# Order of VectorE's steps in a software-pipelined cross attention: the maximum ahead of the normalisation, the product and the reciprocal ahead of the next inputs

## The chip, the cores and the metric

The kernel runs on one core of one Trainium2 chip. The metric is the device time of one execution in microseconds. The core's engines are TensorE (PE, matrix products; PEld is its weight load), VectorE (DVE), ScalarE (ACT), GpSimd (POOL) and SyncE (SP, which here only issues DMAs). Each runs its own instructions in program order and waits on semaphores for the others.

## The reference

The kernel computes a decoder of four layers, each with an attention part, a cross attention part and a feed-forward part. The change lies in the cross attention of layer 2. Cut to what matters:

```python
def _div_clamp_fp8(x, scale):
    y = jnp.clip(x.astype(jnp.float32) / scale, -448.0, 448.0)
    return _fp8_roundtrip(y.astype(jnp.bfloat16).astype(jnp.float32))

ln_out = _ln(hidden_states, ln_w, ln_b)
q = _ln(linear(ln_out, wq), qln_w, qln_b)        # 16 heads of 128
k = _ln(linear(ln_out, wk), kln_w, kln_b)        # 8 heads
v = linear(ln_out, wv)
core = _gqa(q, k, v)                             # softmax(q k) v, two query heads per key head
qx = _ln(linear(ln_out, wqx), qxln_w, qxln_b)
kx, vx = split(einsum(cond, w_kv_x)); kx = _ln(kx, kxln_w, kxln_b)
xout = _gqa(qx, kx, vx)
cat = concatenate([core, xout])
catq = _div_clamp_fp8(cat, proj_smooth)
return einsum(catq, wproj) * (proj_in_scale * proj_w_scale)
```

The batch is 8 and there are 128 positions of 256 features each.

## The kernel before, in words

The cross attention of layer 2 is a loop of 64 blocks: 8 batch elements, and for each of them 4 groups of heads of the self part and 4 of the cross part. A block has four query heads and two key heads, of 128 x 128 values each. Nothing is scheduled by a planner: each engine has its own loop `for i in range(67)`, written out by hand, and iteration `i` of each works on blocks `i`, `i-1`, `i-2` and `i-3` at different stages. The steps and their lines (of the kernel before):

- TensorE, iteration `i`, in this order: `L2x_project(i)` (q L4190, or L4185 in six of the first 16 blocks, k L4194 or L4196, v L4202 or L4204), `L2x_pTr(i-2)` (transposes of the probabilities, L4230), `L2x_scores(i-1)` (L4222), `L2x_pv(i-2)` (probabilities by values, L4238), `L2x_proj(i-3)` (output projection, L4253), `L2x_qkTr(i)` (transposes of normalised q and k, L4210 and L4214), and once in eight iterations `L2x_uTr` (L4048). `L2x_project(i)` waits for `L2x_norm(i-1)`, `L2x_proj(i-3)` for `L2x_cat(i-3)`, `L2x_qkTr(i)` for `L2x_norm(i)`, `L2x_pv(i-2)` for `L2x_smooth(i-3)`, whose buffer it overwrites.
- ScalarE, iteration `i`: `L2x_qkT(i-1)` (L1995, L1997), `L2x_squares(i)` (L1963, L1965), `L2x_vc(i)` (L1971), `L2x_pTc(i-2)` (L2011), `L2x_rstd(i)` (L1975, L1979), `L2x_exp(i-1)` (L2004, four exponentials with their sums).
- GpSimd, iteration `i`: `L2x_cat(i-3)` (the second half of the rounding, L1336 and L1338), `L2x_prob(i-1)` (probabilities by the reciprocal of their sum, L1330), in four of eight iterations `L2x_quantise_sum` (L1321, L1324, L1326). In the first 19 iterations it also splits weights into bf16 parts, one instruction on 128x1024 values in each of 16 of them (`L2x_rest`, `L2x_lo`, `L2x_qx_rest`, `L2x_qx_lo`: L1288, L1293, L1342, L1346).
- VectorE, iteration `i`: `L2x_smooth(i-3)`, `L2x_resid` (once in eight), `L2x_ss(i)` (sum of squares, L3089), `L2x_norm(i)` (L3095, L3096), `L2x_max(i-1)` (L3100), then the work for the next batch element: at `i % 8 == 0` `L2x_stats`, at 1 `L2x_u`, at 3, 4, 5 and 6 one `L2x_quantise` (L2975, L2979, L2981, L2983); last `L2x_recip(i-1)` (L3106). I call the iterations with `L2x_quantise` quantising iterations; there are 28.

In the kernel before, `L2x_smooth` is four instructions: the product of the attention's output with the reciprocal of the smoothing scale (L3111, out of PSUM), the clip to bf16 (L3115), the exponent's bits (L3117) and the rounding constant (L3119). `L2x_cat` on GpSimd adds and subtracts that constant. `L2x_ss(i)` waits for `L2x_squares(i)`, `L2x_norm(i)` for `L2x_rstd(i)`, `L2x_max(i-1)` for `L2x_scores(i-1)`, `L2x_recip(i-1)` for `L2x_exp(i-1)`, the product for `L2x_pv` of its block.

Of the kernel before, what the change touches and what calls it, by code (L numbers as in the profile page):

```python
# [108 lines left out]
def build_program(nc, dram, out_d):  # L109
# [89 lines left out]
    with stack:  # L199
# [2174 lines left out]
        def _(dve):  # L2374
# [716 lines left out]
            def L2x_norm(i):  # L3091
                dve.wait_ge(rstd_done, L2x_start['rstd'] + i + 1)
                if i > 0:
                    dve.wait_ge(kT_done, i)
                dve.tensor_tensor(qk[:, 0:4, :], L2x_q[:, :, :], rstd[:, 0:4].unsqueeze(2).to_broadcast([128, 4, 128]), ALU.mult)  # L3095
                dve.tensor_tensor(qk[:, 4:6, :], L2x_k[:, :, :], rstd[:, 4:6].unsqueeze(2).to_broadcast([128, 2, 128]), ALU.mult).then_inc(norm_done, 1)  # L3096

            def L2x_max(i):
                dve.wait_ge(score_done, L2x_start['score'] + i + 1)
                dve.tensor_reduce(smax[:, :], L2x_s[:, :, :], AX.X, ALU.max, negate=True).then_inc(max_done, 1)  # L3100

            def L2x_recip(i):
                dve.wait_ge(exp_done, L2x_start['exp'] + i + 1)
                if i > 0:
                    dve.wait_ge(prob_done, L2x_start['prob'] + i)
                dve.reciprocal(erec[:, :], esum[:, :]).then_inc(recip_done, 1)  # L3106

            def L2x_smooth(i):
                c = 4 * (i % 8)
                dve.wait_ge(o_done, L2x_start['o'] + i + 1)  # L3110
                dve.tensor_tensor(ratio[:, :, :], L2x_o[:, :, :], smr[:, c:c + 4].unsqueeze(2).to_broadcast([128, 4, 128]), ALU.mult).then_inc(smooth_done, 1)  # L3111
                dve.wait_ge(smooth_done, i + 1)
                if i > 0:
                    dve.wait_ge(cat_done, L2x_start['cat'] + i)
                dve.tensor_scalar(o16[:, :, :], ratio[:, :, :], 448.0, -448.0, ALU.min, ALU.max).then_inc(oclip_done, 1)  # L3115
                dve.wait_ge(oclip_done, i + 1)
                dve.tensor_scalar(oe16u[:, :, :], o16u[:, :, :], 0x7F80, None, ALU.bitwise_and).then_inc(oexpo_done, 1)  # L3117
                dve.wait_ge(oexpo_done, i + 1)
                dve.tensor_scalar(omagic[:, :, :], oe16[:, :, :], 2.0 ** -6, 1.5 * 2.0 ** 20, ALU.max, ALU.mult).then_inc(omagic_done, 1)  # L3119
# [8 lines left out]

            for i in range(67):
                if i >= 3:  # L3130
                    L2x_smooth(i - 3)
                if i >= 11 and (i - 3) % 8 == 0:
                    L2x_resid((i - 11) // 8)
                if i < 64:
                    L2x_ss(i)
                    L2x_norm(i)
                if 1 <= i < 65:
                    L2x_max(i - 1)
                if i < 56:
                    n, s = i // 8 + 1, i % 8  # L3140
                    if s == 0:
                        L2x_stats(n)
                    if s == 1:
                        L2x_u(n)
                    if s in (3, 4, 5, 6):
                        L2x_quantise(4 * n + s - 3)
                if i == 56:
                    L2f_stats(0)
                if i == 57:
                    L2f_u(0)  # L3150
                if i == 60:
                    L2f_stats(1)
                if i == 62:
                    L2f_u(1)
                if 1 <= i < 65:
                    L2x_recip(i - 1)
            L2x_resid(7)

            dve.wait_ge(resid_done, L2x_start['resid'] + 8)
# [1702 lines left out]
```

## Time and profile before

| | |
|---|---|
| median of 3 runs | 2069.88 us (2068.64 to 2070.6) |
| the profiled execution: its time, its span | 2064.8 us, 2062.9 us |
| busy in the span: PE, DVE, ACT, POOL | 87%, 70%, 53%, 55% |
| the loop of the change: first and last start of L3095 (one per iteration) | 808.3 us, 1315.0 us |
| granted TensorE clock from 816 to 1336 us | 1.00 |

The span is the time from the first to the last instruction of one profiled execution. Times of rows are microseconds from the span's start. Of the whole kernel only the stretch from about 808 to 1336 us runs the loop that the change touches. An instruction's duration in a timeline is from its start to its end, so what it waits for after it has started is in it; what it waits for on a semaphore before it starts is idle time of its engine, shown in square brackets with who ended it.

### The profile page before, as it was taken

What the parts mean: (1) busy time and instruction counts of PE and PEld (TensorE: products, weight loads), DVE (VectorE), ACT (ScalarE), POOL (GpSimd) and SP (SyncE); (2) the same over time, 40 slices, a digit from 0 to 9 for tenths busy, and PEclk for the clock granted to TensorE, in tenths of its full rate; (3) what the DMA queues carried; (4) which work ended last, traced back from release to release, by engine and by line L of the source; (5) the groups of instructions that cost most, each with busy time, mean ns of one, the idle gap of its engine ahead of it and who ended that gap; (6) DMA issues with size and microseconds to landing.
All of it is one profiled execution on the core that took longest, in us unless ns stands there. A gap on an engine that the chain in (4) does not pass through costs nothing.

```text
span 2062.9 us, 29936 instructions
## 1 busy us (share of the span) xinstructions
PE 1795.1 (87%) x10766; PEld 1290.9 (63%) x10810; DVE 1451.8 (70%) x2366; ACT 1092.4 (53%) x2325; POOL 1142.0 (55%) x837
## 2 busy tenths in 40 slices
PE   6777789799999896888999999968888888898999
PEld 4111148555565574666777777767777665677887
DVE  5788853456554584777777777589999887867563
ACT  4444431245323264666666666567767656755443
POOL 3799940112595174766555555499999952123221
PEclk9788899689999998999999999989999989999999
DMA  4211001040200010000000000200000002000000
GB/s 157 58 36 36 0 1 54 26 184 21 109 15 21 0 33 18 14 1 1 1 1 1 1 1 31 93 4 1 1 1 1 26 1 84 1 1 1 6 9 9
DMA packets 20395, 54.79 MB, mean 27 GB/s; under 512 B 8095, under 2 KB 11848, under 8 KB 17944
## 3 DMA queue, kind: packets, MB, share of 16 engines
q1 hardware_dynamic: 20248, 52.88, 7.7%
q8 instruction: 87, 1.43, 0.3%
q14 instruction: 60, 0.49, 0.1%
HBM read 44.48 MB, written 1.05 MB: 22 GB/s over the span
## 4 chain that ended last, share of the span: by engine, by line
PE 51%; DVE 21%; ACT 12%; POOL 7%; issue 7%; DMA 0%; DVEq 0%; POOLq 0%; ACTq 0%
DVE sbuf L2446 4%; PE psum L4355 3%; PE psum L4013 3%; ACT sbuf L2004 2%; PE psum L3996 2%; PE psum L3988 2%; PE psum L3641 2%; PE psum L4253 2%; PE psum L4190 2%; ACT sbuf L2100 2%; POOL sbuf L1152 1%; DVE sbuf L3117 1%; PE psum L4663 1%; PE psum L4345 1%; POOL sbuf L1338 1%
## 5 line engine op out<-in xcount | busy, mean ns | idle before, releaser
L1388 POOL TENSOR_TENSOR sbuf<-sbuf 128x1035 f32<-128x1035 f32 x128 | 245.1, 1945 | 0.9 <-ACT sbuf L2068 0.9
L4355 PE MATMUL psum<-sbuf 128*128 128x128 f32 (+1 forms) x1024 | 144.2, 291 | 56.2 <-ACT sbuf L2100 41.4
L2100 ACT ACTIVATE sbuf<-sbuf 128x1001 f32<-128x1001 f32 (+1 forms) x128 | 142.0, 1142 | 84.9 <-DVE sbuf L3241 60.9
L4355 PEld LDWEIGHTS psum<-sbuf 128*128 128x128 f32 (+1 forms) x1024 | 125.9, 152 | 77.5 <-ACT sbuf L2100 55.5
L1330 POOL TENSOR_TENSOR sbuf<-sbuf 128x512 f32<-128x512 f32 x64 | 66.7, 1042 | 172.8 <-DVE sbuf L3106 172.8
L1152 POOL TENSOR_TENSOR sbuf<-sbuf 128x1024 f32<-128x1024 f32 x64 | 149.8, 2353 | 17.0 <-DVE sbuf L2446 17.0
L2446 DVE TENSOR_TENSOR_SCAN sbuf<-psum,sbuf 128x1024 f32<-128x1024 f32 x64 | 144.8, 2278 | 12.6 <-ACT psum L1534 7.4
L2004 ACT ACTIVATE sbuf<-psum,sbuf 128x128 f32<-128x128 f32 x256 | 90.4, 365 | 107.2 <-DVE sbuf L3100 107.2
L3233 DVE SCALAR_TENSOR_TENSOR psum<-sbuf,psum 128x1024 f32<-128x1024 f32 (+1 forms) x96 | 122.3, 1274 | 23.0 <-PE psum L4345 16.5
L3587 PE MATMUL psum<-sbuf 96*128 96x512 bf16 x256 | 82.1, 432 | 60.5 <-DVE sbuf L2446 32.4
L1534 ACT ACTIVATE psum<-psum,sbuf 128x1016 f32<-128x1016 f32 x64 | 69.0, 1082 | 119.7 <-PE psum L3587 119.7
L4253 PE MATMUL psum<-sbuf 128*128 128x256 bf16 x768 | 94.9, 273 | 30.9 <-POOL sbuf L1338 30.5
L3241 DVE TENSOR_TENSOR sbuf<-psum,sbuf 128x1024 f32<-128x1024 f32 (+1 forms) x96 | 116.4, 1212 | 3.3
L4253 PEld LDWEIGHTS psum<-sbuf 128*128 128x128 bf16 x768 | 70.8, 98 | 60.2 <-POOL sbuf L1338 51.4
L3587 PEld LDWEIGHTS psum<-sbuf 96*128 96x128 bf16 x256 | 18.8, 102 | 137.1 <-DVE sbuf L2446 62.4
L1336 POOL TENSOR_TENSOR sbuf<-sbuf 128x512 f32<-128x512 bf16 x64 | 74.5, 1164 | 46.2 <-DVE sbuf L3119 44.5
L1462 POOL TENSOR_TENSOR sbuf<-sbuf 128x1024 f32<-128x1024 f32 x16 | 30.8, 1944 | 120.1 <-DVE sbuf L3437 120.1
L4190 PE MATMUL psum<-sbuf 128*128 128x512 bf16 x304 | 81.7, 387 | 6.1 <-issue 3.9
L1338 POOL TENSOR_TENSOR sbuf<-sbuf 128x512 bf16<-128x512 f32 x64 | 81.3, 1270 | 5.0
L3620 PE MATMUL psum<-sbuf 128*32 128x512 f32 x256 | 78.5, 746 | 3.9 <-POOL sbuf L1152 3.9
L1396 POOL TENSOR_TENSOR sbuf<-sbuf 128x1024 f32<-128x1024 f32 (+1 forms) x32 | 68.7, 2148 | 21.0 <-DVE sbuf L3233 21.0
L3095 DVE TENSOR_TENSOR sbuf<-psum,sbuf 128x512 f32<-128x512 f32 x64 | 44.2, 691 | 50.6 <-ACT sbuf L1979 50.6
(696 smaller groups left out, 5023.0 us busy)
## 6 DMA issues: line engine op xcount, KB each, us to landing
sbuf<-sbuf SPq DMA_DIRECT2D x50, 128.0 KB, 2.4
sbuf<-w_gu_d SPq DMA_DIRECT2D x2, 2048.0 KB, 11.4
sbuf<-w_p_d SPq DMA_DIRECT2D x8, 512.0 KB, 3.6
sbuf<-w_qkv_d SPq DMA_DIRECT2D x3, 768.0 KB, 4.3
sbuf<-w_e_d SPq DMA_DIRECT2D x1, 2048.0 KB, 9.2
sbuf<-w_dn_d SPq DMA_DIRECT2D x1, 2048.0 KB, 18.7
sbuf<-w_q_d SPq DMA_DIRECT2D x1, 2048.0 KB, 7.9
sbuf<-w_qx_d SPq DMA_DIRECT2D x1, 2048.0 KB, 12.4
```

Of the source, the lines that this page charges most:

```text
L1152: pool.tensor_tensor(L0a_hc[i % 4][:, :], L0a_hs[i % 2][:, :], L0a_Cr[g % 4][:, :], ALU.mult).then_inc(hc_done, 1)
L1338: pool.tensor_tensor(cat16[:, :, :], cat[:, :, :], omagic[:, :, :], ALU.subtract).then_inc(cat_done, 1)
L1388: pool.tensor_tensor(P_r[g % 7][:, :, :], rows.unsqueeze(2).to_broadcast([128, 23, 45]), cols.unsqueeze(1).to_broadcast([128, 23, 45]), AL ...
L2004: last = act.activation(prob[:, h, :], L2x_s[:, h, :], ACT.Exp, bias=smax[:, h:h + 1], accum_out=esum[:, h:h + 1])
L2100: act.activation(Q_r[g % 6][:, 0:w], Q_r[g % 6][:, 0:w], ACT.Silu, scale=q8_p[n % 2][:, h:h + 1]).then_inc(silu_done, 1)
L2446: dve.tensor_tensor_scan(L0a_hs[i % 2][:, :], L0a_dAf[i % 2][:, :], L0a_us[i % 3][:, :], 0.0, ALU.mult, ALU.add).then_inc(scan_done, 1)
L3233: dve.scalar_tensor_tensor(M[:, 0:w], Pf_r[g % 7][:, o:o + w], t8_p[n % 2][:, h, 7:8], zps[:, 0:w], ALU.is_ge, ALU.mult).then_inc(mask_don ...
L3241: dve.tensor_tensor(Q_r[g % 6][:, 0:w], Mps[:, 0:w], Pf_r[g % 7][:, o:o + w], ALU.mult).then_inc(prod_done, 1)
L3587: last = pe.matmul(out[:, 512 * h:512 * h + 512], rows, L0a_stack[g % 4][0:96, a, 512 * h:512 * h + 512], start=True, stop=True)
L4190: last = pe.matmul(L2x_q[:, :, :], xs16[n % 2][:, part, c, :], (L2x_q_part, L2x_qx_part)[part](p, g)[:, c, :], start=c == 0 and p == 0, st ...
L4253: last = pe.matmul(L2x_out[:, :], cat16[:, h, :], w_p3[p][:, 4 * (i % 8) + h, :], start=i % 8 == 0 and h == 0 and p == 0, stop=i % 8 == 7 ...
L4355: last = pe.matmul(Gps[0:m, c, :], Q_r[g % 6][:, 128 * c:128 * c + m], ident[:, :], start=h == 0 and c % 4 == 0, stop=h == 7, skip_group_c ...
```

## The change

On VectorE alone, two things are done. `L2x_smooth` is cut in two: the product stays in `L2x_smooth`, and the clip, the exponent's bits and the constant become `L2x_magic`. And the order within an iteration is new. No instruction is added or removed, no wait is added or removed, and no other engine's program is touched; no DMA is issued in the moved steps.

```diff
@@ L2x_smooth(i) @@
                 dve.wait_ge(o_done, L2x_start['o'] + i + 1)
                 dve.tensor_tensor(ratio[:, :, :], L2x_o[:, :, :], smr[:, c:c + 4].unsqueeze(2).to_broadcast([128, 4, 128]), ALU.mult).then_inc(smooth_done, 1)
+
+            def L2x_magic(i):
                 dve.wait_ge(smooth_done, i + 1)
                 if i > 0:
                     dve.wait_ge(cat_done, L2x_start['cat'] + i)
@@ the loop @@
             for i in range(67):
                 if i >= 3:
-                    L2x_smooth(i - 3)
+                    L2x_magic(i - 3)
                 if i >= 11 and (i - 3) % 8 == 0:
                     L2x_resid((i - 11) // 8)
                 if i < 64:
                     L2x_ss(i)
-                    L2x_norm(i)
                 if 1 <= i < 65:
                     L2x_max(i - 1)
+                if i < 64:
+                    L2x_norm(i)
+                if 2 <= i < 66:
+                    L2x_smooth(i - 2)
+                if 1 <= i < 65:
+                    L2x_recip(i - 1)
                 if i < 56:
                     n, s = i // 8 + 1, i % 8
                     ...
                 if i == 62:
                     L2f_u(1)
-                if 1 <= i < 65:
-                    L2x_recip(i - 1)
```

The `...` stands for the work for the next batch element, which is unchanged. In the changed kernel the clip, the exponent's bits and the constant stand two lines further down: L3117, L3119 and L3121.

VectorE in iteration 2, which has no quantisation, from the normalisation up to the constant; before:

```order
L3095 TENSOR_TENSOR sbuf<-psum,sbuf 128x512
L3096 TENSOR_TENSOR sbuf<-psum,sbuf 128x256
L3100 TENSOR_REDUCE sbuf<-psum 128x4
L3106 RECIPROCAL sbuf<-sbuf 128x4
L3111 TENSOR_TENSOR sbuf<-psum,sbuf 128x512
L3115 TENSOR_SCALAR sbuf<-sbuf 128x512
L3117 TENSOR_SCALAR sbuf<-sbuf 128x512
L3119 TENSOR_SCALAR sbuf<-sbuf 128x512
```

The same iteration in the changed kernel:

```order
L3100 TENSOR_REDUCE sbuf<-psum 128x4
L3095 TENSOR_TENSOR sbuf<-psum,sbuf 128x512
L3096 TENSOR_TENSOR sbuf<-psum,sbuf 128x256
L3111 TENSOR_TENSOR sbuf<-psum,sbuf 128x512
L3106 RECIPROCAL sbuf<-sbuf 128x4
L3117 TENSOR_SCALAR sbuf<-sbuf 128x512
L3119 TENSOR_SCALAR sbuf<-sbuf 128x512
L3121 TENSOR_SCALAR sbuf<-sbuf 128x512
```

The maximum (L3100) now stands before the normalisation, and the product (L3111) before the reciprocal (L3106), so that the clip follows the reciprocal directly.

VectorE in a quantising iteration; before:

```order
L3095 TENSOR_TENSOR sbuf<-psum,sbuf 128x512
L3096 TENSOR_TENSOR sbuf<-psum,sbuf 128x256
L3100 TENSOR_REDUCE sbuf<-psum 128x4
L2975 TENSOR_TENSOR sbuf<-sbuf 128x256
L2979 TENSOR_SCALAR sbuf<-sbuf 128x256
L2981 TENSOR_SCALAR sbuf<-sbuf 128x256
L2983 TENSOR_SCALAR sbuf<-sbuf 128x256
L3106 RECIPROCAL sbuf<-sbuf 128x4
L3111 TENSOR_TENSOR sbuf<-psum,sbuf 128x512
L3115 TENSOR_SCALAR sbuf<-sbuf 128x512
L3117 TENSOR_SCALAR sbuf<-sbuf 128x512
L3119 TENSOR_SCALAR sbuf<-sbuf 128x512
```

The same in the changed kernel:

```order
L3100 TENSOR_REDUCE sbuf<-psum 128x4
L3095 TENSOR_TENSOR sbuf<-psum,sbuf 128x512
L3096 TENSOR_TENSOR sbuf<-psum,sbuf 128x256
L3111 TENSOR_TENSOR sbuf<-psum,sbuf 128x512
L3106 RECIPROCAL sbuf<-sbuf 128x4
L2975 TENSOR_TENSOR sbuf<-sbuf 128x256
L2979 TENSOR_SCALAR sbuf<-sbuf 128x256
L2981 TENSOR_SCALAR sbuf<-sbuf 128x256
L2983 TENSOR_SCALAR sbuf<-sbuf 128x256
L3117 TENSOR_SCALAR sbuf<-sbuf 128x512
L3119 TENSOR_SCALAR sbuf<-sbuf 128x512
L3121 TENSOR_SCALAR sbuf<-sbuf 128x512
```

The four quantising instructions (L2975 to L2983) stood between the maximum and the reciprocal; now they stand between the reciprocal and the clip.

## Rows read from the trace of the kernel before

**Rows 1.** Busy time in 64 us of the loop's later part (view of windows).
```profile
core 0: us, PE busy (x) PEld busy (x) DVE busy (x) ACT busy (x) POOL busy (x), PEclk, DMA share, GB/s
1016.00:1080.00 64.00, 61.16 (x397) 49.44 (x403) 48.28 (x96) 42.45 (x141) 33.94 (x32) 1.00 0.00 1
```

**Rows 2.** Waits, 888 to 1330 us: total, times, longest.
```profile
DVE sbuf L3106 <- ACT sbuf L2004: 51.2, 55, 1.6
DVE sbuf L3095 <- ACT sbuf L1979: 42.8, 55, 1.0
PE psum L4253 <- POOL sbuf L1338: 23.4, 32, 2.4
```

**Rows 3.** Timeline of VectorE: the normalisation in iterations 1, 17, 18, 20, 32, 40.
```profile
816.06 0.69 DVE L3095 TENSOR_TENSOR sbuf<-psum,sbuf 128x512 f32<-128x512 f32 x1 [0.61 <-ACT sbuf L1979]
...
957.43 0.69 DVE L3095 TENSOR_TENSOR sbuf<-psum,sbuf 128x512 f32<-128x512 f32 x1 [0.61 <-ACT sbuf L1979]
...
966.27 0.69 DVE L3095 TENSOR_TENSOR sbuf<-psum,sbuf 128x512 f32<-128x512 f32 x1 [0.61 <-ACT sbuf L1979]
...
983.37 0.69 DVE L3095 TENSOR_TENSOR sbuf<-psum,sbuf 128x512 f32<-128x512 f32 x1 [0.61 <-ACT sbuf L1979]
...
1076.79 0.69 DVE L3095 TENSOR_TENSOR sbuf<-psum,sbuf 128x512 f32<-128x512 f32 x1 [0.99 <-ACT sbuf L1979]
...
1138.76 0.69 DVE L3095 TENSOR_TENSOR sbuf<-psum,sbuf 128x512 f32<-128x512 f32 x1 [0.99 <-ACT sbuf L1979]
```

**Rows 4.** Chain that ended last: TensorE through iteration 34, without a wait.
```profile
1087.19 1.24 PE psum L4190 x5
...
1090.59 0.89 PE psum L4222 x8
...
1092.41 1.48 PE psum L4253 x12
1093.89 0.44 PE psum L4210 x4
1094.32 0.22 PE psum L4214 x2
```

**Rows 5.** Timeline, reciprocal of iteration 34, then quantising iteration 35.
```profile
1094.88 0.18 DVE L3106 RECIPROCAL sbuf<-sbuf 128x4 f32<-128x4 f32 x1 [1.57 <-ACT sbuf L2004]
...
1099.44 0.69 DVE L3095 TENSOR_TENSOR sbuf<-psum,sbuf 128x512 f32<-128x512 f32 x1 [0.94 <-ACT sbuf L1979]
...
1100.38 0.68 DVE L3100 TENSOR_REDUCE sbuf<-psum 128x4 f32<-128x512 f32 x1
...
1102.63 0.18 DVE L3106 RECIPROCAL sbuf<-sbuf 128x4 f32<-128x4 f32 x1 [0.32 <-ACT sbuf L2004]
...
1102.89 1.04 POOL L1330 TENSOR_TENSOR sbuf<-sbuf 128x512 f32<-128x512 f32 x1 [3.05 <-DVE sbuf L3106]
...
1103.42 0.79 DVE L3115 TENSOR_SCALAR sbuf<-sbuf 128x512 bf16<-128x512 f32 x1
...
1103.89 0.85 POOL L1321 TENSOR_TENSOR sbuf<-sbuf 128x256 f32<-128x256 bf16 x1
...
1104.25 0.65 DVE L3117 TENSOR_SCALAR sbuf<-sbuf 128x512 uint16<-128x512 uint16 x1
...
1104.82 0.73 POOL L1326 TENSOR_TENSOR sbuf<-sbuf 128x256 bf16<-128x256 f32 x1
...
1104.93 0.90 DVE L3119 TENSOR_SCALAR sbuf<-sbuf 128x512 f32<-128x512 bf16 x1
...
1108.48 1.48 PE L4253 MATMUL psum<-sbuf 128*128 128x256 bf16 x12 [1.07 <-POOL sbuf L1338]
```

**Rows 6.** Timeline, VectorE's iteration 16: GpSimd's 128x1024 split.
```profile
953.19 2.16 POOL L1346 TENSOR_TENSOR sbuf<-sbuf 128x1024 bf16<-128x1024 f32 x1
```

**Rows 7.** Single lines over the loop: durations in ns, min/median/max.
```profile
L3115 DVE TENSOR_SCALAR sbuf<-sbuf x64: 426/793/1429, 828.9 to 1328.6; 128x512 bf16<-128x512 f32 x64
...
L3117 DVE TENSOR_SCALAR sbuf<-sbuf x64: 293/646/2108, 829.7 to 1329.0; 128x512 uint16<-128x512 uint16 x64
...
L2975 DVE TENSOR_TENSOR sbuf<-sbuf x32: 411/415/707, 790.1 to 1248.5; 128x256 f32<-128x256 f32 x32
...
L4185 PE MATMUL psum<-sbuf x24: 592/592/596, 836.9 to 935.9; 128*128 128x512 f32 x24
```

## The prediction, made before the changed kernel ran

> **What bounds the loop now.** I read the windows first. In the later part of the loop TensorE is busy 61.16 of 64 us and VectorE 48.28 [rows 1]: TensorE is nearly full, but not quite. The chain that ended last shows what a full TensorE means: iteration 34 runs from 1087.19 to the end of its last transposes at 1094.54 without a wait, so 7.35 us, about 7.40 with the step to the next [rows 4]. Against this stand the measured periods. From iteration 32 to 40 the normalisation moves from 1076.79 to 1138.76, 61.97 us or 7.75 an iteration; from 1 to 20 it takes 983.37 - 816.06 = 167.3 us, 8.81 an iteration; from 17 to 18 it is 8.84 [rows 3]. So the floor is some 59.3 us for eight iterations, and the loop pays 2.6 us over it later on and far more in the first 20.
>
> The waits say who holds TensorE up: the output projection waits for GpSimd's second half of the rounding (23.4 us in all), and GpSimd is late because VectorE is. VectorE in turn stands still twice in an iteration with nothing else to do: 42.8 us in 55 iterations for the inverse deviation ahead of the normalisation, 51.2 us for the exponentials ahead of the reciprocal [rows 2]. VectorE's own circle (squares, wait, normalisation, maximum, exponentials, reciprocal, rounding, next squares) thus sets the period, not its busy time. In quantising iteration 35 the constant ends at 1104.93 + 0.90 = 1105.83, 6.39 us after the normalisation began, and the projection starts 2.65 us after that, having waited 1.07 [rows 5].
>
> One more thing is in the rows. The clip, the exponent's bits and the constant don't have one duration. The bits take 0.29 us at best, 0.65 in the median, 2.11 at most; the clip 0.43, 0.79 and 1.43 [rows 7]. They are long when GpSimd works: in iteration 35 the clip ends 0.28 us after GpSimd's L1330 (1103.93), the bits 0.16 after L1321 (1104.74), the constant 0.28 after L1326 (1105.55) [rows 5]; in iteration 16 GpSimd's 128x1024 split takes 2.16 us [rows 6], about the longest time of the bits. I read it as one excluding the other. The product L2975 (two SBUF inputs) does it too, 0.41 against 0.71 [rows 7]. The Trainium skill, "SBUF — State Buffer", section "SBUF: two separate sides", says that a VectorE instruction that uses both ports, or has two SBUF inputs, and a GpSimd instruction take a shared pair of ports in turn, whoever starts first for its whole length; the trace agrees.
>
> **The change, step by step.** No work is added, so all depends on the circles. Times below count from R, the end of the reciprocal.
>
> *Maximum first.* It needs the scores, not the deviation, and takes 0.68 us of the 0.94 us in which VectorE waited [rows 5]. *Product before the reciprocal.* The normalisation occupies 0.94 us up to the next instruction, the product some 0.61 (reciprocal and product together are 0.79, 1102.63 to 1103.42 [rows 5]); together 1.55, and the exponentials keep the reciprocal waiting 1.57 after the maximum in an iteration with no filler [rows 5]. Both are hidden. The risk is that the product waits for `L2x_pv(i-2)`, with the reciprocal queued behind it. TensorE ends that 0.93 us after the scores (1091.48 to 1092.41 [rows 4]), and the product starts 1.6 us after them: free, with 0.7 us to spare. The normalisation starts later, but ends some 1.7 us after the scores, while TensorE still has 0.93 + 1.48 us to go before it needs it.
>
> With this VectorE's own circle no longer holds both idle times. The circle that counts now goes over GpSimd and TensorE and takes two iterations: scores(i-1), maximum, exponentials, reciprocal, rounding(i-2), `cat`, projection, transposes, project(i+2), scores(i+1). Its pieces: scores to R 0.05 + 0.68 + 1.57 + 0.18 = 2.48; R to the end of the constant m; from there to the projection 2.65; projection and transposes 1.48 + 0.44 + 0.22 + 0.04 = 2.18; project to the end of the scores 1091.48 - 1087.19 = 4.29 [rows 4, 5]. Period = (11.60 + m) / 2.
>
> - *No quantisation, no split.* The clip follows the reciprocal at once, before GpSimd's L1330 can begin, and runs in 0.43; L1330 then ends at 1.35, the bits at 1.54, the constant at m = 2.0. Period 6.8, under TensorE's 7.40: TensorE sets it.
> - *Quantisation.* Product L2975 to 0.33, L1330 to 1.3, L2979, L2981, L2983 to 2.0, clip to 2.4, then in turns L1321 to 3.0, bits to 3.15, L1326 to 3.8, constant to 4.1. So m = 4.1, where before it was 1105.83 - 1102.81 = 3.02: the four moved instructions no longer lie in the wait for the exponentials. Period 7.85. If L1330 wins the first turn m is 3.8 and the period 7.70.
> - *128x1024 split, no quantisation* (10 iterations): the split begins at 1.54, ends at 3.5, the constant at 3.8. Period 7.7 to 7.85, in place of 8.84 to 9.2.
> - *Split and quantisation* (3 to 6, and 11): `cat` starts only behind both, near 6.0, and the projection at 8.55. Period (2.48 + 8.55 + 2.18 + 4.29)/2 = 8.75, and with q by L4185 (4 x 0.59 in place of 1.24 [rows 4, 7], half of the 1.1 counting) 9.3.
>
> The sum over iterations 1 to 20: ten periods at 7.85 (78.5), four at 9.3 (37.2), two at 8.4 for L4185 (16.8), two for iteration 11 and its follower (17.5), one more at 7.85: 157.9 against 167.3, so -9.4 us. Each later group of eight: four at 7.85 and four at 7.40 and 0.2 for L4048, 61.2 against 61.97, -0.8; with four and a half groups -3.6. The last, unquantised iterations are at TensorE's pace already: -0.4. Together -13.4 us. Profiled execution 2064.8 -> 2051.4 (span 2062.9 -> 2049.5); the median of the runs lies 5.1 above the profiled time, so 2069.9 - 13.4 = 2056.5.
>
> By the nearest rows without the taking of turns (every instruction at its shortest) m would be 2.3 with a quantisation, and the period 6.95, under 7.40. The page's rule, in which GpSimd and VectorE exclude each other, speaks against this change in its quantising iterations, where it puts more of VectorE's instructions against L1330.
>
> **The rivals.**
> 1. *TensorE sets every period.* For it: the shortest durations [rows 7]. Against: turns seen in iteration 35. 62 iterations at 7.40, 6.6 for L4185 and 1.5 for L4048 make 467, the loop now takes 499: -32, giving 2038. Chance 0.08.
> 2. *Later quantising iterations gain nothing and the first 20 only half*, because GpSimd's split takes its turn ahead of the bits and the constant both: -4 to -6, 2064 to 2066. 0.15.
> 3. *The change doesn't reach the end:* VectorE's waits move and the projection waits as before, 2070 ± 4. For it: with quantisation the new period 7.85 is close to the present ones. 0.10.
> 4. *Slower, by the moved quantisation.* m is the place. Each us more in m costs 0.5 us in 28 iterations, 14 us. The gain of 13.4 is gone when m passes 5.05, which needs one more full GpSimd instruction (1.04 us) between the reciprocal and the constant. At m = 5.4 the time is 2075. Against: GpSimd has only L1330, L1321 and L1326 there. 0.09.
>
> **How the numbers follow.** The forecast circle has 0.58, its own range 2049 (m 3.8, splits cheaper) to 2062. A difference of 0.2% is 4.1 us, about what this measurement can tell. Faster: 0.58 + 0.08 + 0.13 of rival 2 and a little of 3 = 0.80; within 0.2%: 0.11; slower 0.09. The range leaves out most of rival 1 and of rival 4: 2044 to 2069.
>
> **What would show it.** Right: from the normalisation of iteration 1 to that of 20 some 158 us, 20 to 56 in steps of 7.4 and 7.85; the wait before L3095 near nothing, the maximum right after the squares; the clip 0.43 us in iterations without quantisation; in quantising ones the constant ending 4.1 us after the reciprocal, with projections that still wait a few tenths. Wrong: the product waiting for L4238, the reciprocal pushed off by it, the constant more than 5 us behind the reciprocal, or an unchanged wait before L4253.

## The result, and the profile after

| | before | after |
|---|---|---|
| median, with lowest and highest | 2068.82 us, 8 runs (2059.31 to 2070.6) | 2056.23 us, 8 runs (2045.5 to 2058.16) |
| profiled execution: time, span | 2064.8 us, 2062.9 us | 2055.56 us, 2053.8 us |
| from the span's start to the normalisation of iteration 1 | 816.1 us | 820.2 us |
| the loop, normalisation of iteration 1 to that of 63 | 499.0 us | 480.6 us |
| from there (iteration 63) to the end of the span | 747.9 us | 753.0 us |

The changed kernel is faster by 0.58%: the ratio of the times is 0.9942, with a 95% interval of 0.9922 to 0.9963. The loop alone gained 18.4 us, and 5.1 us of them were lost again behind it. The two profiled spans differ by only 9.1 us, because the stretch ahead of the loop, which the change does not touch, took 4.1 us more in the changed kernel's. That stretch varies from execution to execution of one kernel: 811.3 us at a mean granted clock of 0.92 in the trace of max_first below, 822.2 us at 0.90 in that of max_first_again, the same program. Where an iteration stands is read, as in [rows 3], from the start of the normalisation in VectorE's timeline; in the changed kernel these are iterations 1, 20, 32, 40 and 63.

```profile
820.15 0.68 DVE L3095 TENSOR_TENSOR sbuf<-psum,sbuf 128x512 f32<-128x512 f32 x1
...
977.07 0.68 DVE L3095 TENSOR_TENSOR sbuf<-psum,sbuf 128x512 f32<-128x512 f32 x1
...
1068.48 0.68 DVE L3095 TENSOR_TENSOR sbuf<-psum,sbuf 128x512 f32<-128x512 f32 x1
1129.11 0.68 DVE L3095 TENSOR_TENSOR sbuf<-psum,sbuf 128x512 f32<-128x512 f32 x1
...
1300.76 0.68 DVE L3095 TENSOR_TENSOR sbuf<-psum,sbuf 128x512 f32<-128x512 f32 x1
```

Iterations 1 to 20 take 156.9 us (before 167.3, [rows 3]), 32 to 40 take 60.63 (before 61.97). The square bracket of [rows 3], the wait of the normalisation for the inverse deviation, is gone from the rows: the maximum now fills that time. VectorE's wait in an iteration has moved to the maximum itself, which waits for the scores. In the view of waits, 880 to 1316 us (total, times, longest), this reads so:

```profile
DVE sbuf L3100 <- PE psum L4227: 35.3, 46, 1.1
...
PE psum L4258 <- POOL sbuf L1338: 14.5, 18, 2.7
```

The projection's wait for GpSimd (L4258, in the kernel before L4253, 23.4 us in 32 cases [rows 2]) is down to 14.5 us in 18. The chain that ended last shows both kinds of iteration. First, from 1078.02, an iteration that TensorE sets, without a wait; then the quantising iteration 35, where the chain leaves TensorE for VectorE's maximum when the scores are there (1089.95), and comes back to TensorE only with a later projection:

```profile
1078.02 1.24 PE psum L4195 x5
...
1083.25 1.31 PE psum L4258 x12
...
1084.99 0.22 PE psum L4219 x2
...
1089.95 0.70 DVE sbuf L3100
```

The TensorE iteration takes 1085.21 - 1078.02 + 0.05 = 7.24 us. I had taken 7.40: the projection was 1.48 us in [rows 4] and is 1.31 here, where `cat` is ready before TensorE comes to it. The iteration of [rows 4] was not quite free of waits: the timeline of the weight loads has the projection's first one begin only with its matmuls, at 1092.40, after 0.39 us of waiting for L1338. The rounding of iteration 35 in the timeline of VectorE and GpSimd is the forecast sequence:

```profile
1092.21 0.18 DVE L3106 RECIPROCAL sbuf<-sbuf 128x4 f32<-128x4 f32 x1
1092.31 0.41 DVE L2975 TENSOR_TENSOR sbuf<-sbuf 128x256 f32<-128x256 f32 x1
...
1092.47 1.15 POOL L1330 TENSOR_TENSOR sbuf<-sbuf 128x512 f32<-128x512 f32 x1 [3.23 <-DVE sbuf L3106]
...
1092.75 1.02 DVE L2979 TENSOR_SCALAR sbuf<-sbuf 128x256 bf16<-128x256 f32 x1
...
1094.28 0.42 DVE L3117 TENSOR_SCALAR sbuf<-sbuf 128x512 bf16<-128x512 f32 x1
1094.44 0.78 POOL L1321 TENSOR_TENSOR sbuf<-sbuf 128x256 f32<-128x256 bf16 x1 [0.82 <-DVE sbuf L2983]
1094.73 0.65 DVE L3119 TENSOR_SCALAR sbuf<-sbuf 128x512 uint16<-128x512 uint16 x1
...
1095.30 0.73 POOL L1326 TENSOR_TENSOR sbuf<-sbuf 128x256 bf16<-128x256 f32 x1
1095.41 0.90 DVE L3121 TENSOR_SCALAR sbuf<-sbuf 128x512 f32<-128x512 bf16 x1
```

The constant (L3121) ends at 1096.31, 3.92 us after the reciprocal (1092.39); L2979, whose shortest duration in this trace is 0.29 us, takes 1.02 because it started behind L1330.

### The profile page after: what moved, and what is told of

The parts are those of the page before. It is cut to its first block, busy times and chain, and to the rows that moved or that the text cites. A ratio compares the mean times of both kernels' runs of the same rounds, so it can differ in the third digit from the quotient of the medians.

```text
span 2053.8 us, 29936 instructions
## 1 busy us (share of the span) xinstructions
PE 1803.1 (88%) x10766; PEld 1306.0 (64%) x10810; DVE 1465.0 (71%) x2366; ACT 1098.5 (53%) x2325; POOL 1145.8 (56%) x837
## 4 chain that ended last, share of the span: by engine, by line
PE 60%; DVE 17%; ACT 9%; POOL 7%; issue 6%; DMA 0%; DVEq 0%; POOLq 0%; ACTq 0%
DVE sbuf L2446 4%; PE psum L4360 4%; PE psum L4258 3%; PE psum L3993 3%; PE psum L4001 3%; PE psum L4018 3%; PE psum L4195 2%; PE psum L3646 2%; PE psum L4227 2%; PE psum L4668 1%; ACT sbuf L2004 1%; ACT sbuf L2100 1%; POOL sbuf L1388 1%; PE psum L4369 1%; PE psum L4350 1%
## 5 line engine op out<-in xcount | busy, mean ns | idle before, releaser
L4360 PE MATMUL psum<-sbuf 128*128 128x128 f32 (+1 forms) x1024 | 150.5, 300 | 54.4 <-ACT sbuf L2100 39.6
L4360 PEld LDWEIGHTS psum<-sbuf 128*128 128x128 f32 (+1 forms) x1024 | 132.8, 158 | 74.0 <-ACT sbuf L2100 52.8
L1330 POOL TENSOR_TENSOR sbuf<-sbuf 128x512 f32<-128x512 f32 x64 | 72.2, 1128 | 131.7 <-DVE sbuf L3106 129.8
L4258 PE MATMUL psum<-sbuf 128*128 128x256 bf16 x768 | 95.8, 275 | 20.2 <-POOL sbuf L1338 20.0
L4258 PEld LDWEIGHTS psum<-sbuf 128*128 128x128 bf16 x768 | 72.9, 98 | 44.0 <-POOL sbuf L1338 32.1
L1336 POOL TENSOR_TENSOR sbuf<-sbuf 128x512 f32<-128x512 bf16 x64 | 74.4, 1162 | 37.2 <-DVE sbuf L3121 35.5
L3089 DVE TENSOR_REDUCE sbuf<-sbuf 128x6 f32<-128x768 f32 x64 | 60.8, 950 | 44.8 <-ACT sbuf L1965 44.7
L1338 POOL TENSOR_TENSOR sbuf<-sbuf 128x512 bf16<-128x512 f32 x64 | 81.2, 1269 | 5.0
```

Of the source, the lines that this page charges most:

```text
L1338: pool.tensor_tensor(cat16[:, :, :], cat[:, :, :], omagic[:, :, :], ALU.subtract).then_inc(cat_done, 1)
L4258: last = pe.matmul(L2x_out[:, :], cat16[:, h, :], w_p3[p][:, 4 * (i % 8) + h, :], start=i % 8 == 0 and h == 0 and p == 0, stop=i % 8 == 7 ...
L4360: last = pe.matmul(Gps[0:m, c, :], Q_r[g % 6][:, 128 * c:128 * c + m], ident[:, :], start=h == 0 and c % 4 == 0, stop=h == 7, skip_group_c ...
```

## The experiments

I call the parts A (the maximum ahead of the normalisation), B (`L2x_smooth` cut in two, with the product ahead of the clip by one iteration) and C (the reciprocal ahead of the next inputs' work). The changed kernel is A + B + C. All lengths in this table are read as above, each from one profiled execution; times in us. m is, as in the prediction, the time from the end of the reciprocal to the end of the constant, and a circle is a closed chain of waits through the engines that fixes the loop's period. The ratio is to the kernel before, run on the same chip.

| kernel | parts | median | ratio, 95% interval | 1 to 20 | 20 to 56 | 56 to 63 | loop | loop to end |
|---|---|---|---|---|---|---|---|---|
| before | none | 2068.82 | | 167.3 | 279.3 | 52.3 | 499.0 | 747.9 |
| changed | A B C | 2056.23 | 0.9942 [0.9922, 0.9963] | 156.9 | 272.8 | 50.9 | 480.6 | 753.0 |
| after_again | A B C | 2057.06 | 0.9942 [0.9926, 0.9959] | 157.0 | 272.8 | 50.9 | 480.7 | 753.0 |
| max_first | A | 2045.79 | 0.9874 [0.9848, 0.9899] | 154.2 | 268.8 | 50.9 | 473.9 | 749.0 |
| max_first_again | A | 2045.16 | 0.9872 [0.9850, 0.9895] | 154.2 | 268.8 | 50.9 | 473.9 | 749.1 |
| recip_last | A B | 2048.26 | 0.9893 [0.9871, 0.9915] | 156.4 | 271.3 | 50.9 | 478.6 | 747.7 |
| no_max_first | B C | 2100.98 | 1.0145 [1.0122, 1.0168] | 174.1 | 301.8 | 53.6 | 529.6 | 748.3 |
| product_early | B | 2063.06 | 0.9966 [0.9954, 0.9978] | 165.5 | 274.2 | 51.4 | 491.1 | 749.4 |
| quantise_early | A B C, quantisation moved | 2084.68 | 1.0065 [1.0044, 1.0085] | 172.5 | 290.0 | 50.9 | 513.4 | 746.8 |
| bits_twice | A B C, one instruction more | 2059.66 | 0.9951 [0.9934, 0.9967] | 160.7 | 276.6 | 50.9 | 488.2 | 747.9 |
| mixed | A, and B where nothing is quantised | 2044.26 | 0.9870 [0.9849, 0.9891] | 155.6 | 268.8 | 50.9 | 475.4 | 747.5 |
| leave_later | A B C, 24 instructions behind the loop | 2052.76 | 0.9912 [0.9896, 0.9929] | 156.9 | 272.8 | 50.9 | 480.6 | 748.7 |

### One part at a time: max_first, recip_last, no_max_first

max_first is the kernel before with A alone:

```diff
                 if i < 64:
                     L2x_ss(i)
-                    L2x_norm(i)
                 if 1 <= i < 65:
                     L2x_max(i - 1)
+                if i < 64:
+                    L2x_norm(i)
```

> The kernel before with one part of the change: the maximum ahead of the normalisation; product, clip, bits and constant stay together, the reciprocal stays last. Theory (the circle scores, maximum, reciprocal, cat, projection over two iterations): VectorE's own circle loses its wait before the normalisation; in quantising iterations the reciprocal ends about 3.2 us after the scores and the constant 3.0 after it, period 7.7; without quantisation TensorE's pace. From the normalisation of iteration 1 to that of 63 some 481 us against 499 before, so nearly the whole gain of the change, -15 to -19 us. Rival (each moved step brings its own share): about half, some -6 to -10 us.

recip_last is the changed kernel without C:

```diff
                 if 2 <= i < 66:
                     L2x_smooth(i - 2)
-                if 1 <= i < 65:
-                    L2x_recip(i - 1)
                 if i < 56:
                     ...
+                if 1 <= i < 65:
+                    L2x_recip(i - 1)
```

> The changed kernel with the reciprocal again behind the quantisation (maximum first and early product stay). Theory: reciprocal 3.6 us after the scores in quantising iterations, constant 2.4 after it, but cat has to wait for GpSimd's two quantising additions, projection 5.6 after the reciprocal: period 7.8, against 7.76 in the changed kernel. So no difference of over 2 us from the changed kernel, 1 to 63 some 482 us. Rival (the reciprocal's place matters, since it starts GpSimd): 8 us or more worse than the changed kernel.

no_max_first is the changed kernel without A:

```diff
                 if i < 64:
                     L2x_ss(i)
+                    L2x_norm(i)
                 if 1 <= i < 65:
                     L2x_max(i - 1)
-                if i < 64:
-                    L2x_norm(i)
```

> The changed kernel with the normalisation again ahead of the maximum; product early, reciprocal ahead of the quantisation. Theory: VectorE's own circle is whole again (squares, wait, normalisation, maximum, exponentials, reciprocal 3.37 us after the normalisation's start, then 3.9 to the constant in quantising iterations, then 1.47 to the next normalisation): 8.7 us in each quantising iteration, 7.3 in the others. 1 to 63 some 509 us, 10 us more than before: about +0.5%. Rival (the other moves help by themselves): -3 to -8 us against before.

A alone takes 25.1 us from the loop, more than the whole change does and 6 us more than the most I expected of it: its four quantising iterations from 27 to 31 take 30.31 us, 7.58 each in place of the expected 7.7, and the others go at 7.24. B on top of it costs 4.7 us and C 2.0 more (473.9, 478.6, 480.6). In the medians A alone is ahead of the changed kernel by 10 to 12 us, and recip_last by 8 to 9, more than the loop gives, because the stretch behind the loop is shorter than in the changed kernel as well (749.0 and 747.7 us against 753.0; see below). Its quantising iteration 35 in the timeline of VectorE and GpSimd shows why:

```profile
1076.86 0.69 DVE L3100 TENSOR_REDUCE sbuf<-psum 128x4 f32<-128x512 f32 x1 [0.80 <-PE psum L4223]
1077.46 0.68 DVE L3095 TENSOR_TENSOR sbuf<-psum,sbuf 128x512 f32<-128x512 f32 x1
...
1078.84 0.29 DVE L2979 TENSOR_SCALAR sbuf<-sbuf 128x256 bf16<-128x256 f32 x1
...
1079.64 0.17 DVE L3106 RECIPROCAL sbuf<-sbuf 128x4 f32<-128x4 f32 x1
...
1079.89 1.04 POOL L1330 TENSOR_TENSOR sbuf<-sbuf 128x512 f32<-128x512 f32 x1 [3.38 <-DVE sbuf L3106]
1080.42 0.80 DVE L3115 TENSOR_SCALAR sbuf<-sbuf 128x512 bf16<-128x512 f32 x1
...
1081.93 0.90 DVE L3119 TENSOR_SCALAR sbuf<-sbuf 128x512 f32<-128x512 bf16 x1
```

The quantisation lies in the time of the exponentials, GpSimd stands still, and L2979 takes 0.29 us in place of 1.02. The reciprocal is later for it, 1079.81 - 1076.82 = 2.99 us after the scores in place of 2.48, but the constant follows it by 3.02 in place of 3.9. The circle of the prediction with these two in it is 2.99 + 3.02 + 2.65 + 2.18 + 4.29 = 15.13 us for two iterations; the normalisations of iterations 35 and 37 (1077.46 and 1092.62) start 15.16 apart.

In recip_last the same circle reads so in the chain (from the scores of a quantising iteration to its projection):

```profile
1101.91 0.03 DVE sbuf L3100
...
1105.29 0.18 DVE sbuf L3106
...
1105.54 1.13 POOL sbuf L1330
1106.67 0.68 POOL sbuf L1321
...
1107.43 0.79 POOL sbuf L1326
1108.22 1.13 POOL sbuf L1336
...
1110.74 1.48 PE psum L4258 x12
```

With the product and the quantisation both ahead of it, the reciprocal ends 3.59 us after the scores (1105.46 - 1101.87). The clip runs early and the constant is ready 2.18 us behind the reciprocal, but that is of no use: `cat` (L1336) begins only when GpSimd has done L1330, L1321 and L1326, after some 2.7 us. From the scores to `cat` it is 2.99 + 3.10 = 6.09 us with A, 3.59 + 2.72 = 6.31 with A and B, and 2.48 + 4.00 = 6.48 with all three (1092.39 to 1096.39). With the 2.56 + 2.18 + 4.29 us of the rest, two iterations should take 15.12, 15.34 and 15.51 us; measured are 15.16, 15.38 and 15.53. From iteration 20 to 56 there are ten such circles of two iterations, so these differences make 2.2 us for B and 1.7 for C, where 2.5 and 1.5 are measured.

Without A, the order B + C is 30.6 us slower in the loop than the kernel before, where I had expected 10: the product stands between the maximum and the reciprocal, and the reciprocal ahead of the quantisation, so that a quantising iteration has both of VectorE's waits and the whole quantisation one behind the other. Most quantising iterations take 8.74 us, as expected (8.7); what I had too low are others: of those expected at 7.3, 24 to 25 takes 8.30 and 26 to 27 takes 8.10. Its timeline has the wait in front of the normalisation in full again, here in iterations 32 and 40, 67.29 us apart:

```profile
1096.32 0.69 DVE L3095 TENSOR_TENSOR sbuf<-psum,sbuf 128x512 f32<-128x512 f32 x1 [0.98 <-ACT sbuf L1979]
...
1163.61 0.69 DVE L3095 TENSOR_TENSOR sbuf<-psum,sbuf 128x512 f32<-128x512 f32 x1 [0.99 <-ACT sbuf L1979]
```

### The product alone: product_early

The kernel before with `L2x_smooth` cut in two, `L2x_magic(i-3)` first and `L2x_smooth(i-2)` behind the maximum; the reciprocal stays last, the normalisation first.

```diff
                 if i >= 3:
-                    L2x_smooth(i - 3)
+                    L2x_magic(i - 3)
                 ...
                 if 1 <= i < 65:
                     L2x_max(i - 1)
+                if 2 <= i < 66:
+                    L2x_smooth(i - 2)
```

> The kernel before with the product alone moved: behind the maximum, ahead of quantisation and reciprocal; normalisation still ahead of the maximum. Theory: VectorE's own circle is 3.37 to the reciprocal's end, 1.84 (2.2 with quantisation) to the constant and 1.47 to the next normalisation, 6.7 to 7.0, below TensorE's pace, so this alone also frees it; but with quantisation cat comes behind GpSimd's two additions, 5.5 after the reciprocal, and the circle through the projection is (3.45 + 5.5 + 2.18 + 4.55)/2 = 7.85. 1 to 63 some 483 us, -14 to -16 us. Rival (only the maximum's place matters): within 3 us of the kernel before.

B without A gains 7.9 us in the loop, half of what I expected of it. In unquantised iterations the constant ends 1.84 us after the reciprocal in place of 2.19. In quantising ones the reciprocal comes 0.2 us later, and the constant 2.17 us after it in place of 3.02 (of the 20 from iteration 19 on, one still has 3.02). So B gains while VectorE still waits for the deviation, and loses 4.7 us with A in place, where, as above, the late reciprocal costs more than B gives.

### Where the quantisation should lie: quantise_early

The changed kernel with the quantisation moved from behind the reciprocal to behind the constant, ahead of the squares, so that m has no quantisation in it:

```diff
                 if i >= 11 and (i - 3) % 8 == 0:
                     L2x_resid((i - 11) // 8)
+                if i < 56 and i % 8 in (3, 4, 5, 6):
+                    L2x_quantise(4 * (i // 8 + 1) + i % 8 - 3)
                 if i < 64:
                     L2x_ss(i)
                 ...
-                    if s in (3, 4, 5, 6):
-                        L2x_quantise(4 * n + s - 3)
```

> The changed kernel with the four quantising instructions moved from behind the reciprocal to behind the constant, ahead of the sum of squares, where VectorE stands idle 0.7 to 1.2 us for the squares and 0.8 for the scores. Theory: the constant then ends some 2.5 us after the reciprocal instead of 3.9, cat is held by GpSimd's own additions to a projection 5.6 us after the reciprocal, period of quantising iterations about 7.3 instead of 7.76. 1 to 63 some 471 us against 480.6: 9 us better than the changed kernel. Rival (the sum of squares becomes late, and with it the inverse deviation and the normalisation): no gain or a loss of some us.

I expected 471 us for the loop; it takes 513.4, 32.8 us more than in the changed kernel. m is 2.20 us in quantising iterations, no longer than expected; the loss is at the new place. The timeline of both engines at the new place:

```profile
1063.38 0.94 DVE L2975 TENSOR_TENSOR sbuf<-sbuf 128x256 f32<-128x256 f32 x1
1064.00 1.35 POOL L1336 TENSOR_TENSOR sbuf<-sbuf 128x512 f32<-128x512 bf16 x1
...
1064.36 1.14 DVE L2979 TENSOR_SCALAR sbuf<-sbuf 128x256 bf16<-128x256 f32 x1
...
1065.43 1.26 POOL L1338 TENSOR_TENSOR sbuf<-sbuf 128x512 bf16<-128x512 f32 x1
1065.54 1.24 DVE L2981 TENSOR_SCALAR sbuf<-sbuf 128x256 uint16<-128x256 uint16 x1
...
1066.81 0.29 DVE L2983 TENSOR_SCALAR sbuf<-sbuf 128x256 f32<-128x256 bf16 x1
1067.02 0.95 DVE L3089 TENSOR_REDUCE sbuf<-sbuf 128x6 f32<-128x768 f32 x1
```

Three instructions of 0.41, 0.29 and 0.23 us at their shortest take 0.94, 1.14 and 1.24, as each has one of GpSimd's in front of it, and the squares come 1067.02 - 1063.38 = 3.64 us after the quantisation began. The period there is 9.05 us (the maximum starts at 1058.83 and at 1067.88 in this trace). This is the statement of the Trainium skill, "SBUF — State Buffer", section "SBUF: two separate sides", that GpSimd's instructions and those of VectorE that use both ports or have two SBUF inputs take a shared pair of ports in turn; the trace agrees, with 1.24 against 0.23 us for L2981. I had used it for the moved rounding and not for this place.

### The size of m: bits_twice

The changed kernel with the exponent's bits taken twice, one behind the other (not shown: one wait behind the loop counts the 64 more):

```diff
                 dve.tensor_scalar(oe16u[:, :, :], o16u[:, :, :], 0x7F80, None, ALU.bitwise_and).then_inc(oexpo_done, 1)
-                dve.wait_ge(oexpo_done, i + 1)
+                dve.wait_ge(oexpo_done, 2 * i + 1)
+                dve.tensor_scalar(oe16u[:, :, :], o16u[:, :, :], 0x7F80, None, ALU.bitwise_and).then_inc(oexpo_done, 1)
+                dve.wait_ge(oexpo_done, 2 * i + 2)
```

> The changed kernel with the exponent's bits taken twice in each iteration (the same result), which adds some 0.3 us to VectorE between the reciprocal and the constant, everywhere. Theory (the circle over two iterations, and only where its sum exceeds TensorE's pace): 0 in iterations without quantisation after number 20 (there is 0.8 us of slack), about 0.15 in quantising ones, so eight iterations 61.2 instead of 60.6 and 1 to 63 some 5 us more, 485 us. Rival (VectorE's busy time counts in each iteration): 0.3 in each of 62, 19 us more.

From iteration 13 on m grows by 0.33 us (3.90 to 4.24 with a quantisation, 1.84 to 2.17 without). A usual group of eight, 24 to 32, grows from 60.36 to 61.24 us. These 0.88 us are about five times half of 0.34: the four quantising iterations and the one right behind them (31 to 32, 7.24 to 7.46), which closes the last circle of two. The other unquantised iterations keep their length (24 to 26 at 7.24 each), so TensorE sets them, and the last seven take 50.9 as before. This is the prediction's rule that a microsecond in m costs half of one in quantising iterations and nothing in the others, but for the one iteration behind each group. The stretch from 32 to 40 grows by 0.61 only, because in the changed kernel it is longer than its neighbours (60.63): m is 4.19 there in iteration 36 by itself. From 20 to 56 all this makes the measured 3.8 us. In iterations 3, 4, 5 and 11, where GpSimd splits weights too, m is 6.04 us in place of 3.9, and 12 to 13 is shorter (9.97 in place of 11.49, see the last section); the net of 1 to 20 is another 3.8. The loop so costs 7.6 us more where I expected 5, and not the rival's 19.

### The better order in each iteration: mixed

recip_last, but with the product behind the reciprocal, as in the kernel before, in the quantising iterations:

```diff
+                late = i < 56 and i % 8 in (3, 4, 5, 6)
-                if 2 <= i < 66:
+                if 2 <= i < 66 and not late:
                     L2x_smooth(i - 2)
                 ...
                 if 1 <= i < 65:
                     L2x_recip(i - 1)
+                if late:
+                    L2x_smooth(i - 2)
```

> A version meant to be best: maximum first, reciprocal last (behind the quantisation, which so stays in the wait for the exponentials), the product ahead of the reciprocal only in iterations without quantisation. Theory (circle over two iterations): with a 128x1024 split and no quantisation the constant comes 3.64 after the reciprocal, as in the changed kernel, instead of 4.01 in the kernel with the maximum first alone; with quantisation 3.0, as there. So iteration 1 to 20 some 152 us against 154.2, the rest alike (268.8 and 50.9), 1 to 63 some 472 us against 473.9 and 480.6; median 2044 us. Rival (mixing costs the product's slot once at each change of order): 474 to 476 us.

The loop takes 475.4 us, 1.5 more than with A alone; from 20 to 56 the two are equal (268.8). I expected 472, with 2 us saved by B while GpSimd splits weights. It saves only 0.3 there, and 1.7 are lost in one place: iterations 11 to 13 take 18.75 us against 17.02 in max_first, with 11.48 against 9.09 from 12 to 13. By its median mixed is not to be told from max_first. No version beat A alone by more than the measurement can tell.

### Why the end came later: after_again, max_first_again, leave_later

after_again and max_first_again are the same programs again, to see whether the loop and the stretch behind it repeat.

> The changed kernel once more, beside the others on one chip. In the first comparison 7 of 8 of its runs had a granted clock of 0.939 or 0.940 over the whole kernel (2055 to 2058 us), one had 0.947 (2045.5 us). Theory (the clock of the stretches outside the loop varies from run to run and is no work of the change): here the clock spreads as with the kernel before, 0.944 to 0.950, and the time is 2050 us. Rival (the change lowers the clock outside the loop): 0.940 and 2056 us again. The loop takes 480.6 us from the normalisation of iteration 1 to that of 63 in either case.

> The kernel before with the maximum first alone, once more. In the loop it is 6.7 us shorter than the changed kernel (473.9 against 480.6). If the clock outside the loop is the same for both, the difference of the medians is 7 us; if the changed kernel's clock is lower by itself, 10 to 12 us as in the first comparisons.

They do: 480.7 and 473.9 us in the loop, 753.0 and 749.1 behind it. My theory for after_again, 2050 us with a clock that spreads as before, fell: all its six runs stand at 0.938 to 0.940 and 2056 to 2057 us, as the rival said, and its median is 11.9 us above max_first_again's. So the 5.1 us that the changed kernel loses behind the loop are no accident of one execution. No instruction there is different. The windows of the changed kernel behind the loop (columns as in [rows 1]):

```profile
1300.00:1700.00 400.00, 329.57 (x2159) 285.13 (x2158) 338.51 (x513) 254.31 (x383) 337.42 (x182) 0.91 0.05 16
1700.00:2053.00 353.00, 324.90 (x2554) 257.42 (x2554) 221.75 (x354) 193.23 (x351) 88.42 (x72) 0.98 0.03 10
```

The same two stretches behind the loop of the kernel before:

```profile
1315.00:1715.00 400.00, 324.41 (x2166) 277.39 (x2164) 340.66 (x517) 257.31 (x386) 337.39 (x182) 0.93 0.06 20
1715.00:2062.00 347.00, 321.94 (x2550) 255.31 (x2546) 218.77 (x349) 189.60 (x346) 88.41 (x72) 0.99 0.02 5
```

The granted clock (third number from the end) is 0.91 and 0.98 where it was 0.93 and 0.99, and TensorE is busy longer with about as many matmuls. leave_later tests whether the work or the moment matters: it is the changed kernel with 24 more instructions of VectorE between the loop and its last addition (not shown: one later wait counts them).

```diff
+            dve.wait_ge(omagic_done, 64)
+            for r in range(24):
+                dve.wait_ge(oexpo_done, 64 + r)
+                dve.tensor_scalar(oe16u[:, :, :], o16u[:, :, :], 0x7F80, None, ALU.bitwise_and).then_inc(oexpo_done, 1)
+            dve.wait_ge(oexpo_done, 88)
             L2x_resid(7)
```

> The changed kernel with 24 repeats of the last block's exponent bits before the last residual addition, so that the loop's end comes some 4 us later and all behind it moves by that; the loop itself stays at 480.6 us. In the changed kernel's two profiles the stretch from the normalisation of iteration 63 to the end takes 753.0 us, in all others 747 to 749, at a higher clock. Theory (the clock behind the loop depends on when the loop is left): the stretch takes 749 + 4 = 753 us or less, mean clock 0.944 or more, median within 2 us of the changed kernel's 2057 although 4 us of work were added. Rival (the changed kernel's loop, with its power, lowers the clock behind it, whenever it is left): 753 + 4 = 757 us, clock 0.939, median 2061.

The first instruction of the next stage on GpSimd, in the timelines of the changed kernel and of leave_later:

```profile
1327.31 5.75 POOL L1388 TENSOR_TENSOR sbuf<-sbuf 128x1035 f32<-128x1035 f32 x3 [0.92 <-ACT sbuf L2068]
```

```profile
1330.95 1.93 POOL L1388 TENSOR_TENSOR sbuf<-sbuf 128x1035 f32<-128x1035 f32 x1 [0.91 <-ACT sbuf L2068]
```

It comes 26.55 us after the last normalisation in the one (1300.76) and 28.36 in the other (1302.59). The work was added and the stage does start 1.8 us later, not the 4 that I had expected. Yet from there to the end the changed kernel takes 2053.8 - 1327.31 = 726.5 us and leave_later 2051.3 - 1330.95 = 720.4, on the same instructions, with this clock:

```profile
1302.00:1702.00 400.00, 323.15 (x2158) 276.70 (x2157) 349.56 (x539) 255.92 (x384) 337.29 (x182) 0.93 0.06 18
1702.00:2051.00 349.00, 322.71 (x2554) 255.79 (x2554) 219.62 (x352) 191.01 (x349) 88.41 (x72) 0.98 0.02 7
```

A kernel with more to do is 3.5 to 4.3 us faster in the median, where I expected it within 2 us of the changed one; the intervals of the ratios just overlap. The rival, that the changed loop lowers the clock behind it whenever it is left, gave 757 us from the last normalisation to the end; it is 748.7. bits_twice, which also does more, has 747.9. So the 5 us are not what the change does to the later stages, which run the same instructions: they go with the clock granted there.

What brings that clock about these runs don't show. It is not the delay of the next stage alone: in mixed the same instruction of GpSimd also comes 26.55 us after the last normalisation (1322.07), and from there to the end it takes 720.9 us. It is not the time since the span's start alone either: max_first and max_first_again leave the loop at 1285.2 and 1296.1 us and both take 749 us from there.

## Why the prediction was right, and where only its numbers met

The time, 2056.23 us, is the forecast 2056.5, inside the range, with the forecast sign. The terms behind it were further off, and that the total met is luck: the loop gained 5.0 us more than forecast, and 5.1 us were lost behind it, where the forecast had nothing.

- **What bounds the loop:** right. The two waits of VectorE set the period, and A, which fills one of them, is worth 25.1 us alone; without it the rest makes the kernel slower.
- **"Maximum first", "product before the reciprocal", both hidden:** the first is right. Of the second I asked only whether the product waits or delays the reciprocal, and it does neither (R is 2.48 us after the scores, as worked out). What I didn't weigh is what the whole change would be without it. The parts B and C are a loss of 6.7 us in the loop beside A: B delays the reciprocal where something is quantised, and C puts the quantisation's 2 us behind it, where L1330 lengthens L2979 to 1.02. The term m = 4.1 had this in it, so the forecast didn't suffer; I never asked whether one part spoke against another.
- **The two-iteration circle:** right. m was forecast at 4.1 or 3.8 and is 3.9 in quantising iterations (but 5.0 in iteration 12 and 4.19 in 36); it was forecast at 2.0 and is 1.84 to 2.3 in the others of the later part. Two quantising iterations take (2.48 + 3.90 + 2.65 + 2.18 + 4.29) = 15.50 us by the formula and 7.24 + 8.29 = 15.53 in the trace. max_first, and bits_twice behind iteration 20, moved as the formula says.
- **TensorE's pace of 7.40:** mis-sized; it is 7.24. The projection's 1.48 us of [rows 4] is what it takes when its weight load has waited for `cat`; with `cat` there in time it is 1.31.
- **The sum:** the terms were -9.4, -3.6 and -0.4 us; measured are -10.4, -6.5 and -1.4. Of the 5.0 us that the forecast gave too little, 3.9 lie behind iteration 20. Some 2.9 of them are TensorE's pace in the 24 unquantised iterations there, and 1.1 the 19 quantising ones at 7.79 in place of 7.85. The other 1.0, in the first 20, is a net: iterations 3 to 6 take 35.6 us in place of 37.2, iteration 11 and its follower 18.7 in place of 17.5, where the granted clock fell once (last section), and the rest 0.5 less.
- **What lies behind the loop:** taken as unchanged, and 5.1 us longer at a lower granted clock. This undid the surplus almost exactly. Without the loss behind the loop the prediction would have stood some 5 us too high, still inside its range.
- **The profiled execution and the median:** the forecast put the profiled time at 2051.4 us and it is 2055.56; the median is 0.7 us above it and not 5.1. The 4.1 us that the stretch ahead of the loop took more make most of that difference: the 5.1 belonged to one execution of the kernel before, so that the profiled time's miss is not one of the circle. One of the eight runs of the changed kernel took 2045.5 us at a granted clock of 0.947, the seven others 2055 to 2058 at 0.939 or 0.940. There is no trace of it. The two profiled executions of max_first and max_first_again lie as far apart, 2035.91 us at 0.951 and 2046.97 at 0.944, and theirs is ahead of the loop (811.3 and 822.2 us); so that run is no evidence on the loss behind the loop.
- **The rivals:** 1 (TensorE sets every period, 2038) fell on the 8.29 us of every second quantising iteration. 2 fell: iterations 20 to 56 gained 6.5 us, and with them most of what the forecast had too little. 3 fell, the projection's wait is shorter by 9 us and the loop by 18.4. 4 needed m above 5.05; it stays at 3.9 in all but two iterations (5.0 and 4.19). quantise_early shows its mechanism at another place.

## What to carry to other kernels

In a loop over several engines write down each circle with its waits, and for a change of several parts work out each part alone and not only their sum: here one moved step of 0.68 us was worth 25 us in 63 iterations, and the two others took 7 back. Filler work belongs into the time in which one's own engine waits and the engine that shares its port stands still too; the same four instructions cost about 1.2 us there and 3.6 us beside GpSimd's additions. A gain read from one stage is not yet the gain of the kernel: compare the rest of the span as well, with its granted clock.

## What was not expected of the hardware

- **A stall of a few microseconds in the loop can cost the clock.** In the changed kernel, iteration 12 to 13 takes 11.49 us; before it took 9.82, in max_first 9.09. The projection waits behind GpSimd's 128x1024 split, and when it comes, in the timeline, its 12 matmuls last 2.74 us in place of 1.48:

```profile
909.12 2.31 POOL L1346 TENSOR_TENSOR sbuf<-sbuf 128x1024 bf16<-128x1024 f32 x1
...
912.69 1.49 DVE L2975 TENSOR_TENSOR sbuf<-sbuf 128x256 f32<-128x256 f32 x1
...
913.95 2.74 PE L4258 MATMUL psum<-sbuf 128*128 128x256 bf16 x12 [2.73 <-POOL sbuf L1338]
```

  The windows around it give the granted clock: 1.00 up to 912 us, 0.66 in the next 4 us (a mixture of the levels 1.2 and 2.4 GHz), 0.91, and 1.00 again. TensorE had stood still for 2.73 us in front of it.

```profile
908.00:912.00 4.00, 3.22 (x21) 2.61 (x19) 3.94 (x7) 2.82 (x10) 3.92 (x4) 1.00 0.01 2
912.00:916.00 4.00, 2.05 (x10) 1.46 (x11) 3.85 (x7) 0.56 (x4) 3.10 (x4) 0.66 0.00 0
916.00:920.00 4.00, 3.95 (x22) 3.09 (x21) 1.70 (x3) 2.21 (x4) 3.48 (x4) 0.91 0.00 0
920.00:924.00 4.00, 4.00 (x33) 3.58 (x32) 3.14 (x5) 2.84 (x13) 0.35 (x1) 1.00 0.03 6
```

  The clock falls at this projection in every kernel with B, after waits of the projection of 2.14 us (quantise_early) to 3.13 (no_max_first), also in bits_twice and quantise_early, whose step from 12 to 13 is short (9.97 and 9.06) but the one before it long: from 11 to 13 they take 19.33 and 19.98 us, the changed kernel 18.73, max_first 17.02. In max_first the wait is 1.70 us at most and the clock stays at 1.00. But the length of the wait doesn't decide alone: the kernel before waits 2.40 us there and keeps 1.00, mixed waits 2.39 and loses it. What else decides these runs don't show.
- **A kernel with 24 instructions more was the faster one,** by 6.1 us from the start of the next stage to the end (leave_later). The instructions there are the same; the rows differ in the granted clock. Differences of some 5 us in kernels of 2 ms may be of this kind, whatever the change, and between single executions of one kernel 11 us were seen (max_first).
